# A decoder layer on one core: new orders in the key stage, in the turning of the key sums and in the first output steps

## What is computed

```python
# block 1, per batch, 16 heads of 16, 64 features
logits = k @ W0 - 0.5 * sum(k * k)
alpha  = softmax(logits over rows and features, per head)
N, D   = alpha^T @ v,  sum(alpha over rows)
phi    = softmax(q @ W0, over features)
out    = (phi @ N) / (phi @ D + EPS)
# block 3, 8 heads of 64, 8 experts
values = gm[n, e] * (x @ value_experts[e])
out    = softmax(causal(q k^T)) @ values
y      = sum over e, h of gm[n, e] * (out @ output_experts[e, h])
```

## Time and profile before

| what | us |
|---|---|
| median of 3 runs (all) | 1020.06 (1013.84, 1022.8, 1020.06) |
| the profiled execution's own time | 1013.04 |
| its span, first to last instruction | 1011.3 |
| TensorE busy in it | 940.0 |
| VectorE busy | 691.1 |
| ScalarE busy | 391.5 |
| GpSimd busy | 240.6 |

### The profile page before, as it was taken

One profiled execution on the slowest core, in us unless ns is written; L12 is line 12 of the kernel. 1 busy time (PEld: TensorE's weight loads), 2 busy tenths in 40 slices (PEclk: granted clock), 3 DMA queues, 4 the chain that ended last, 5 costly groups with the idle time before them and its releaser, 6 DMA issues.

```text
span 1011.3 us, 14688 instructions
## 1 busy us (share of the span) xinstructions
PE 940.0 (93%) x5620; PEld 728.0 (72%) x5620; DVE 691.1 (68%) x1047; ACT 391.5 (39%) x683; POOL 240.6 (24%) x261
## 2 busy tenths in 40 slices
PE   5888999999998899989999799999999999998997
PEld 3557778887755565689976586888876656558997
DVE  3566567547656878799968575665575767869886
ACT  5334556212456567501113255640205755750000
POOL 6212323113523313146700013210022201411000
PEclk9999999999999999999999999999999999999999
DMA  6113000333143431136640000012221000013663
GB/s 225 29 42 126 1 1 2 120 137 125 46 160 129 146 125 57 38 115 183 205 155 1 1 1 1 2 49 86 81 84 42 22 21 0 28 56 112 181 187 106
DMA packets 33848, 81.56 MB, mean 81 GB/s; under 512 B 5956, under 2 KB 10660, under 8 KB 33780
## 3 DMA queue, kind: packets, MB, share of 16 engines
q1 hardware_dynamic: 32500, 76.44, 23.6%
q10 hardware_dynamic: 1280, 4.20, 1.6%
HBM read 61.26 MB, written 19.20 MB: 80 GB/s over the span
## 4 chain that ended last, share of the span: by engine, by line
PE 75%; DVE 13%; ACT 4%; issue 3%; SPq 2%; DMA 2%; POOL 1%; DVEq 0%; POOLq 0%; ACTq 0%
PE ps L1025 17%; PE ps L1322 10%; PE ps L1259 7%; PE ps L1327 5%; PE ps L1219 5%; PE ps L1174 4%; PE ps L1235 3%; DVE region L919 3%; PE ps L1033 3%; PE ps L1188 3%; PE ps L1137 3%; PE ps L1127 2%; PE ps L1295 2%; PE ps L1296 2%; SPq L297 2%
## 5 line engine op out<-in xcount | busy, mean ns | idle before, releaser
L1259 PE MATMUL ps<-region 128*128 128x512 f32 (+3 forms) x384 | 161.5, 504 | 0.0
L898 DVE TENSOR_REDUCE region<-ps 128x1 f32<-128x512 f32 (+1 forms) x192 | 98.1, 551 | 67.0 <-PE ps L1238 67.0
L700 ACT ACTIVATE region<-ps 128x512 f32<-128x512 f32 x192 | 92.3, 487 | 125.5 <-PE ps L1298 113.8
L1322 PE MATMUL ps<-expert_hi,kst 128*128 128x256 f32 x512 | 124.1, 283 | 9.9 <-DVE kst L973 9.9
L942 DVE COPY_PREDICATED region<-region,ps 128x512 f32<-128x512 uint32 x112 | 82.0, 736 | 71.9 <-PE ps L1025 71.3
L1322 PE MATMUL ps<-expert_lo,kst 128*128 128x256 f32 x512 | 122.8, 280 | 0.0
L1322 PEld LDWEIGHTS ps<-expert_hi,kst 128*128 128x128 f32 x512 | 96.8, 189 | 11.3 <-DVE kst L973 8.9
L513 ACT ACTIVATE region<-ps 64x512 f32<-64x512 f32 (+4 forms) x146 | 80.7, 555 | 59.0 <-PE ps L1137 20.6
L1025 PE MATMUL ps<-expert_hi,wide_hi 128*128 128x512 f32 x256 | 102.6, 401 | 0.0
L1025 PE MATMUL ps<-expert_hi,wide_lo 128*128 128x512 f32 x256 | 100.1, 391 | 0.0
L1025 PE MATMUL ps<-expert_lo,wide_hi 128*128 128x512 f32 x256 | 99.9, 390 | 0.0
(11 more groups left out here) (142 smaller groups left out, 1772.3 us busy)
## 6 DMA issues: line engine op xcount, KB each, us to landing
region<-hot_rows SPq DMA_DIRECT2D x128, 128.0 KB, 3.3
expert_hi<-halves_kept SPq DMA_DIRECT2D x24, 512.0 KB, 3.6
expert_lo<-halves_kept SPq DMA_DIRECT2D x24, 512.0 KB, 5.0
halves_kept<-expert_hi SPq DMA_DIRECT2D x16, 512.0 KB, 2.7
halves_kept<-expert_lo SPq DMA_DIRECT2D x16, 512.0 KB, 3.9
expert<-in_value_experts SPq DMA_DIRECT2D x8, 512.0 KB, 5.1
expert<-in_output_experts SPq DMA_DIRECT2D x8, 512.0 KB, 5.1
gb<-gate_rows ACTq DMA_DIRECT2D x16, 256.0 KB, 4.0
```

The costliest lines, as they stand in the source:

```text
L700: act.activation(PT[:, g % RING, lo:CH], ps[:, 4 + g % 2, 0:CH - lo], ACT.Exp).then_inc(sem["pt_ready"], 1)
L898: dve.tensor_reduce(mx[:, i, at_mx:at_mx + 1], ps[:, max_bank(h, m), 0:w], AX.X, ALU.max).then_inc(sem["s_max"], 1)
L1259: mm(ps[:, SUM_BANK[c], lo:CH], V3[:, j, h // 2, h % 2 * HD3:(h % 2 + 2) * HD3], PT[:, g % RING, lo:CH], start=(j == 0), stop=(j == TC * ( ...
L1322: mm(ps[:, 4 + t // 2, t % 2 * D:(t % 2 + 1) * D], kst[n % 2][:, t * P:(t + 1) * P], w[:, slot, columns], start=(n == 0 and t % 2 == 0 and ...
```

## The change

Key stage: the sums of squares are no longer one piece but are spread behind the values of tiles 1, 2, 5, 6 and 7. In the last tile DVE computes the key weights' input between the maxima and the subtraction, subtracts POOL's maximum ahead of the last value bias, and multiplies in two pieces (heads 0 to 9, heads 10 to 15); PE's two halves of the sums wait for one piece each. ACT exponentiates the key weights ahead of the last tile and of the last query bias. Only the ones that stay are set. W3's halves are rounded behind tiles 2 and 6 in place of 1 and 4. Feature steps: ACT's exponential of query tile 1 stands ahead of its copy of the sums; PE turns the sums ahead of the other transposes of step 2; DVE places them between that step's maxima and its subtraction. Attention's end: ACT copies the sums ahead of the output, and DVE's inversion waits for the first copy only. Output steps: (1,1) stands ahead of (0,3), and `normalise` 6, 7 and 8 stand behind masks 0, 1 and 4.

```diff
-    SUMMED = [(0, 0), (0, 1), (0, 2), (1, 0), (0, 3), (1, 1), (1, 2), (1, 3)]
+    SUMMED = [(0, 0), (0, 1), (0, 2), (1, 0), (1, 1), (0, 3), (1, 2), (1, 3)]
+    FIRST_SUMS = H1 // 2 + 2
+        NORMALISED_AFTER = (0, 1, 4)
+        SQUARES_AT = {1: range(0, 2), 2: range(2, 6), 5: range(6, 10), 6: range(10, 14), 7: range(14, 16)}
...
                 for t in range(TT):
-                    for n in QUERIES_AT.get(t, ()):
+                    queries = QUERIES_AT.get(t, ())
+                    for n in queries[:1]:
                         biased(kqT, n, 7 - n % 2, 0, "q_ps", "q_sb", b)
-
+                    if t == TT - 1:
+                        until(act, "ak_ready", b, 1)
+                        act.activation(ak_all, ak_all, ACT.Exp).then_inc(sem["w_ready"], 1)
                     until(act, "fk_sub", b, t + 1)
                     act.activation(E1[:, t, :], E1[:, t, :], ACT.Exp).then_inc(sem["e_ready"], 1)
-                    if b == 0 and t in (1, 4):
+                    for n in queries[1:]:
+                        biased(kqT, n, 7 - n % 2, 0, "q_ps", "q_sb", b)
+                    if b == 0 and t in (2, 6):
                         i = t // 4
...
                     if s == 1:
+                        features_exp(0, 1)
                         until(act, "n_ps", b, 2)
                         copy(N1T, ps[:, 4, :], "n_sb")
...
+                    copy(rden[own:own + HALF, cs], ps[oth:oth + HALF, SUM_BANK[c], :], "o_sb")
                     copy(oT[own:own + HALF, h // 2, cs], ps[own:own + HALF, SUM_BANK[c], :], "o_sb")
-                    copy(rden[own:own + HALF, cs], ps[oth:oth + HALF, SUM_BANK[c], :], "o_sb")
...
-                step(dve.memset(V1_all, 1.0))
+                dve.memset(V1[:, :, :, HD1:V1W], 1.0).then_inc(sem["v_ones"], 1)
+                dve.memset(V1_all[:, TT * H1 * V1W:], 1.0).then_inc(sem["v_ones"], 1)
...
+                    if t == TT - 1:
+                        until(dve, "mk_ready", b, TT * DA)
+                        key_weights()
...
+                    if t == TT - 1:
+                        until(dve, "k_max_ready", b, 1)
+                        dve.tensor_tensor(ak, ak, k_max.unsqueeze(1).broadcast_to([P, TT, H1]),
+                                          ALU.subtract).then_inc(sem["ak_ready"], 1)
                     until(dve, "v_ps", b, t + 1)
...
+                for hs in (slice(0, FIRST_SUMS), slice(FIRST_SUMS, H1)):
+                    dve.tensor_tensor(V1[:, :, hs, :], V1[:, :, hs, :],
+                                      ak[:, :, hs].unsqueeze(3).broadcast_to([P, TT, hs.stop - hs.start, V1W]),
+                                      ALU.mult).then_inc(sem["wv_ready"], 1)
...
+                        if s == 2:
+                            place_sums()
...
-                    until(dve, "o_sb", b, 2 * (NC * (2 * PARTS[k][0] + 1) + c0 // CH + 1))
+                    until(dve, "o_sb", b, 2 * (NC * (2 * PARTS[k][0] + 1) + c0 // CH) + 1)
...
                 normalise(H3 - 3)
-                normalise(H3 - 2)
...
-                    if n in (1, 3):
-                        normalise(H3 - 1 + n // 2)
+                    if n in NORMALISED_AFTER:
+                        normalise(H3 - 2 + NORMALISED_AFTER.index(n))
...
-                        until(pe, "wv_ready", b, 1)
+                        until(pe, "wv_ready", b, s + 1)
```

More of the change, by code:

```diff
@@ L588, in gates, with features_exp @@
                                    ps[:, GATE_BANK[c], 0:TC * G], ACT.Exp, scale=-1.0).then_inc(sem["gate_exp"], 1)
[L591 to L592 removed]
+                def features_exp(a, t):
+                    wide, scale = (H1 * NF, 1.0) if a == 0 else (K2, SCALE2)
+                    until(act, "f_sub", b, a * TT + t + 1)
+                    act.activation(phi[:, t % 2, 0:wide], phi[:, t % 2, 0:wide], ACT.Exp,
+                                   scale=scale).then_inc(sem["f_exp"], 1)
                 for s in range(LAST):
@@ L762, in _, with key_weights @@
             for b in range(B):
-                step(dve.memset(V1_all, 1.0))
+                dve.memset(V1[:, :, :, HD1:V1W], 1.0).then_inc(sem["v_ones"], 1)
+                dve.memset(V1_all[:, TT * H1 * V1W:], 1.0).then_inc(sem["v_ones"], 1)
+                def key_weights():
+                    until(dve, "kk_ps", b, 1)
+                    step(dve.scalar_tensor_tensor(ak_all, ps[:, 6, 0:TT * H1], -0.5, mk_all, ALU.mult, ALU.add))
+                    dve.tensor_reduce(ak_top, ak.rearrange("p t h -> p h t"), AX.X, ALU.max
+                                      ).then_inc(sem["ak_top_ready"], 1)
                 for t in range(TT):
@@ L784, in _ @@
                                       ALU.add).then_inc(sem["v_sb"], 1)
-                until(dve, "kk_ps", b, 1)
-                step(dve.scalar_tensor_tensor(ak_all, ps[:, 6, 0:TT * H1], -0.5, mk_all, ALU.mult, ALU.add))
-                dve.tensor_reduce(ak_top, ak.rearrange("p t h -> p h t"), AX.X, ALU.max
-                                  ).then_inc(sem["ak_top_ready"], 1)
                 def gates(c):
@@ L1069, in _ @@
                 for t in range(TT):
-                    if t == 1:
-                        until(pe, "kk_sb", b, 1)
-                        for m in range(TT * DA):
-                            last = mm(ps[:, 6, m * 8:m * 8 + 96], kk[:, m % DA, m // DA * P:(m // DA + 1) * P],
-                                      head_of, start=(m == 0), stop=(m == TT * DA - 1), skip_group_check=True)
-                        last.then_inc(sem["kk_ps"], 1)
                     if t >= 2:
@@ L1092, in _ @@
                     last.then_inc(sem["v_ps"], 1)
+                    if t == min(SQUARES_AT):
+                        until(pe, "kk_sb", b, 1)
+                    for m in SQUARES_AT.get(t, ()):
+                        last = mm(ps[:, 6, m * 8:m * 8 + 96], kk[:, m % DA, m // DA * P:(m // DA + 1) * P],
+                                  head_of, start=(m == 0), stop=(m == TT * DA - 1), skip_group_check=True)
+                    if t == max(SQUARES_AT):
+                        last.then_inc(sem["kk_ps"], 1)
                     for n in QUERIES_AT.get(t, ()):
@@ L1130, in _ @@
                         last.then_inc(sem["f_ps"], 1)
+                    if s == 2:
+                        until(pe, "n_sb", b, 1)
+                        for u in range(PAIRS1 // 2):
+                            last = pe.transpose(ps[:, 5, u * P:(u + 1) * P], N1T[:, u * P:(u + 1) * P], ident)
+                        last.then_inc(sem["nT_ps"], 1)
                     for a, t in due(s, 1):
@@ L1140, in _ @@
                     if s == 2:
-                        until(pe, "n_sb", b, 1)
-                        for u in range(PAIRS1 // 2):
-                            last = pe.transpose(ps[:, 5, u * P:(u + 1) * P], N1T[:, u * P:(u + 1) * P], ident)
-                        last.then_inc(sem["nT_ps"], 1)
                         until(pe, "n_blk", b, 2 * len(N1_RUNS))
```

38 lines of the change are left out of this document (16 added, 22 removed).

## The result

| | median us (range, runs) | ratio to the kernel before, 95% interval |
|---|---|---|
| before | 1016.43 (1012.66 to 1022.8, 13) | |
| changed | 1009.71 (1002.33 to 1015.66, 13) | 0.9926, 0.9902 to 0.995 |

The forecast was 1008, with a gain of 11.7. The median is 1.7 us above it, and the gain is 0.74% (0.5 to 1.0%), some 7.5 us. That is under the 1% from which on the prediction speaks of faster: it is the case "same", which had 0.36 there against 0.60 for faster. The kernel before also came out 3.6 us lower over 13 runs than over the first three. Part of the good agreement in absolute time is that accident, so the gain is the better test, and by it 4 us of the 11.7 are missing.

The account below looks back on a forecast made before the run. TensorE, busy for 93% of the span, was taken to bound the kernel, so only its waits and slow-clock stretches could be won. Terms -4.8 - 2.2 + 5.7 - 10.4 = -11.7 us from 1020.06, rounded 1008; range 998 to 1017.

Parts of the forecast that it names:

- faster: Outcome of a measured time under 1009.9 us, at least 1% below the kernel before; chance 0.60.
- same: Outcome of a time that a measurement cannot tell from no change, within 1% or 10.2 us; chance 0.36.
- Part 1: Batch 1's key weights: TensorE's 3.41 us wait and the slow stretch behind it (1.43) go, together 4.8 us gained.
- Part 2: Turned sums in the feature steps: 1.4 us gained in batch 1 and 0.8 in batch 0, together 2.2.
- Part 3: Batch 0's key weights: GpSimd's reduction comes late, sums start 4.1 us later plus 1.6 for the clock, price +5.7 us.
- Rival A: Batch 0's reduction pays only 1.8 us from its release; key-weights term -2.3, not +5.7; time 1000; chance 0.15.
- Part 4: First output steps: 8.7 of 9.9 us of TensorE's waits go, plus 1.7 for the clock, together 10.4 us gained.
- rival B: Output steps give about 5 us, not 10.4; steps 2 and 5 each keep 1.5 us wait per batch; 1013.5; chance 0.16.
- Sum: All terms together: -4.8 - 2.2 + 5.7 - 10.4 = -11.7 us, forecast time 1008; chance 0.64.
- C: After batch 0's 6.4 us pause TensorE stays at 1.2 GHz through the feature steps; 1025 or more; chance 0.05.

Follow-up runs that it names:

- x5: e1 with the old orders of feature steps 1 and 2 (turning, placing of the sums, exponential of query tile 1): 1003.73 us, ratio 0.9848.
- e1: Changed kernel with batch 0's GpSimd reduction set ahead of the second W3 subtraction: 1000.24 us, ratio 0.9828 to the kernel before.
- e2: Changed kernel with W3's second half rounded behind tile 4 in place of tile 6: 1000.16 us, ratio 0.9832 to the kernel before.
- e3: Kernel before with only the new orders of the attention's end and the output steps: 1014.24 us, ratio 0.995.
- y3: Kernel before with batch 0's GpSimd reduction set ahead of its second W3 subtraction: 1011.89 us, ratio 0.9964.
- e4: Changed kernel with the old orders of the attention's end and the output steps: 1014.63 us, ratio 0.9964 to the kernel before.
- x6: e1 with the transposes of the next batch two output steps later: 997.92 us, ratio 0.9797 to the kernel before.
- x7: e1 with the former output table, (0,3) ahead of (1,1) and part 8 inverted behind mask 3: 996.26 us, ratio 0.9788 to the kernel before.
- y1: e1 with both edits of x6 and x7, later transposes and former table: 998.09 us, ratio 0.9823 to the kernel before.
- y2: e2 with the first expert piece split one step earlier and the former output table: 998.5 us, ratio 0.9831 to the kernel before.

## Why the prediction was right or wrong

- **Part 1 (-4.8), right.** Batch 1's wait of 3.41 us is gone, both halves of the sums take 3.71, and TensorE's own queue is what is late. From the first key features to the sums pass 29.4 us in place of 33.0, and behind them the 1.43 of the earlier trace rows went too: 5.0 together.
- **Part 2 (-1.4 and -0.8), right in its layout; its worth is not settled.** The forecast of 5.4 us from sums to numerators is 5.43. I priced it without a slow stretch behind the new pauses, and in batch 1's profiles there mostly is one. x5 puts both batches together at 0.8 to 2.0 us.
- **Part 3 (+5.7), right in mechanism.** Reduction at 70.53 (70.7 forecast), sums at 73.44 (73.45). Rival A, a price of 1.8 us from the release, falls with e1 and e2. Its time of 1000 is what the kernel takes when the wait is removed. The price of the lower clock, for which I added 1.6 us, is 1.79 in the profile. Wrong was that it is new: e3 and y3, with the old key stage, have sums of 6.44 and 6.52 us, so the kernel before mostly pays it too, and only its one profile does not.
- **Part 4 (-10.4), the step that failed.** "9.9 - 1.2 = 8.7 us gained, and 1.7 for the clock" was right in kind and mis-sized; e3 and e4 measure about 4. The profile says where the rest is: the masks still wait 2.5 us and not 1.2; 2.25 us are a new wait for `xn` and 0.87 one for a load, so 9.9 - 2.5 - 2.25 - 0.87 = 4.3; and the slow stretch stays, only 8 us later, so 0 in place of 1.7. I followed VectorE and TensorE alone. GpSimd's chain for the next batch and SyncE's fetch by the table stood behind the same events, and TensorE met them: it now comes to the first transposes 449.10 - 2.25 - 427.63 = 19.2 us behind its first output step, where it came 449.55 - 425.79 = 23.8 us behind it, and of these 4.5 us it waits 2.25. That is near rival B's 5 us, but by another mechanism: the waits that B placed at steps 2 and 5 were 2.5 us in both batches together, not 6, and all of them at step 5.
- **Sum.** -5.0, about -1.5 for both batches' turning, +5.7, -4.3 make -5.1, 2.4 short of the 7.5 measured and at the edge of the interval (5.1 to 10). If the slow stretch of part 3 is taken out, since the kernel before has it as well in two of three traces, part 3 is the 4.1 us by which the sums are later and the sum -6.7; that is an estimate. The steps named explain the profile, not each microsecond of the mean; at full clock the change gives 8.7 us by the means, and 0.9 are lost to the clock. Part 4 was forecast 6 us too large and the rest together 2 us too small, which leaves the 4 us that are missing; that 1008 was met to 1.7 us is the luck of a base that was 3.6 us too high.
- **The base.** The profile before ran at a mean clock of 0.994, where its 23 runs lost 12.8 us on average, which is 0.987. I read its three slow stretches as belonging to their pauses and the rest as free. They are chance in part, and the 7 us between the profile and the median of the runs shown are mostly this: the profile lost 1013.04 x 0.006 = 6.1 us.
- **C** does not hold: the longest time at the lower clock is the 6.9 us between 70 and 78 us, half of them in the pause itself.

The rule of the Trainium skill ("GPSIMD Engine Reference", "Instruction dispatch": the first call to a freshly loaded kernel pays a load of some 6 us, 5.95 measured) fits, with somewhat more here, 6.69 and 6.83 us. e1's 7.13 us, ahead of the ordinary subtraction behind the reduction, shows that the way back costs as much; in e1 and y3 it is hidden.

## What to carry to other kernels

Write the GpSimd queue so that no ordinary operation stands close ahead of a reduction across partitions (7 us here) that a fuller engine waits for; count its price from the end of what stands there, and let it be paid behind work that nobody needs. When an engine that bounds is made earlier, list everything on all queues that it meets in the next ten microseconds (the next batch's tiles and loads too), since the gain is the distance to the nearest of them. And never take the clock's price from one profile: compare the mean clock over the runs.

## What the hardware showed that I had not expected

The spread of some 10 us between runs of one kernel is in large part the clock: in the changed kernel the standard deviation is 3.5 us, with 2.1 at full clock and 2.3 in what is lost. How much is lost differs between kernels: 13.7 us on average there, 5.3 in x6.

The same output step of 24 matmuls takes TensorE one of two times, and keeps to it for a long stretch. Starts of the low-part matmuls (8 per step) in batch 0 of x7:

```profile
450.54 1.07 PE L1361 MATMUL ps<-expert_hi,qq 128*128 128x256 f32 x8
453.26 1.07 PE L1361 MATMUL ps<-expert_hi,qq 128*128 128x256 f32 x8
455.98 1.07 PE L1361 MATMUL ps<-expert_hi,qq 128*128 128x256 f32 x8
```

and in the same place of y1:

```profile
459.13 1.11 PE L1361 MATMUL ps<-expert_hi,qq 128*128 128x256 f32 x8
461.96 1.10 PE L1361 MATMUL ps<-expert_hi,qq 128*128 128x256 f32 x8
```

That is 2.72 and 2.83 us at a granted clock of 1.00. The kernel before has 2.72 in batch 0 from step 6 on and 2.83 in batch 1; the changed kernel has mostly 2.83 in both. Over 26 steps it is 2.9 us, as much as one of the edits here. In batch 0 the changed kernel, e2, e3, y1 and y2 have 2.83 and the other eight 2.72; in batch 1 only e2 and y3 have 2.72. No edit of this study goes with it. Whether it holds for a kernel or changes from run to run I can't tell from one profile of each, so a difference of 3 us at full clock, as that of x7, can be this. What sets it is open.
